# Casting a weight once into scratch inside an earlier phase, and emitting a conv and its transposes per channel chunk

## The reference

```python
xn = _layernorm(x)                       # x: (2, 4096, 2048)
q, k, v = xn@Wq.T+bq, xn@Wk.T+bk, xn@Wv.T+bv
q = dwconv3(q); k = dwconv3(k)           # depthwise, 3 taps along time
kv = k * v
y = irfft(rfft(kv) * rfft(ssm_kernel))   # long causal convolution
attn = ((y + kv*D_skip) * q) @ Wo.T + bo
h = xn @ W1.T                            # 2048 -> 8192
a = gelu(clip(round(h/0.1), -32768, 32767) * 0.1)
out = x + attn + a @ W2.T                # 8192 -> 2048
```

## Time and profile before

| | us |
|---|---|
| time, median of 2 runs | 5781.74 |
| the two runs | 5723.97 and 5839.51 |
| the profiled execution, its own time | 5727.18 |
| its span, slowest of 8 cores (core 4) | 5725.6 |
| spans of the other cores | 5682.0 to 5716.4 |

### The profile page before, as it was taken

How to read it: one execution, slowest core, us unless ns; L and a number is a source line. 1 busy time by engine, 2 the same in 40 slices (tenths; PEclk the granted TensorE clock), 3 DMA queues, 4 the chain that set the end, 5 groups by cost and what they waited for, 6 DMA issues and landing times. The chain is left out here.

```text
span 5725.6 us, 52508 instructions; the slowest of 8 cores (5682.0 to 5725.6 us)
## 1 busy us (share of the span) xinstructions
PE 3493.8 (61%) x18560; PEld 1797.6 (31%) x18560; DVE 1402.9 (25%) x2784; ACT 413.6 (7%) x791; POOL 652.0 (11%) x1212
## 2 busy tenths in 40 slices
PE   3777733999972602747747567514666666555644
PEld 1333312888861200323313223201222222221211
DVE  0111130445450210031031221310276673001011
ACT  0111100222220100000000000000111110000000
POOL 0000010111111000121121121200000001111111
PEclk9898966999986856979978889756899999988988
DMA  8777877122215014867857858341211112333333
GB/s 178 195 192 194 194 202 117 31 38 46 31 16 89 1 21 115 218 172 186 220 147 198 205 148 228 122 89 30 78 48 48 48 52 38 53 57 71 45 68 67
DMA packets 401726, 614.48 MB, mean 107 GB/s; under 512 B 228928, under 2 KB 283200, under 8 KB 371904
## 3 DMA queue, kind: packets, MB, share of 16 engines
q0 software_dynamic: 132320, 420.64, 35.1%
q1 hardware_dynamic: 269152, 190.48, 11.6%
HBM read 578.90 MB, written 138.94 MB: 125 GB/s over the span
## 5 line engine op out<-in xcount | busy, mean ns | idle before, releaser
L815 PE MATMUL ps<-p_kvg,p_tf 128*128 128x512 bf16 x3264 | 760.2, 393 | 523.9 <-DMA p_kvg<-kv_sp 294.7
L1103 PE MATMUL ps<-p_w,p_a 128*128 128x512 bf16 x2048 | 516.4, 400 | 390.5 <-DMA p_w<-w2T 274.0
L360 PE MATMUL ps<-p_ssm,p_tf 128*128 128x512 bf16 x2176 | 530.9, 409 | 241.6 <-ACT p_kb L377 152.6
L1047 PE MATMUL ps<-p_xn,p_w 128*128 128x512 bf16 x2048 | 476.0, 387 | 246.2 <-DVE p_u L1061 211.0
L815 PEld LDWEIGHTS ps<-p_kvg,p_tf 128*128 128x128 bf16 x3264 | 319.6, 100 | 964.1 <-issue 627.8
L533 PE MATMUL ps<-p_xq,p_wk 128*128 128x256 bf16 x3328 | 367.5, 273 | 183.0 <-DMA p_ckb<-ckb 183.0
L1103 PEld LDWEIGHTS ps<-p_w,p_a 128*128 128x128 bf16 x2048 | 192.0, 101 | 715.0 <-issue 549.4
L533 PEld LDWEIGHTS ps<-p_xq,p_wk 128*128 128x128 bf16 x3328 | 326.4, 98 | 222.4 <-issue 183.8
L360 PEld LDWEIGHTS ps<-p_ssm,p_tf 128*128 128x128 bf16 x2176 | 222.0, 104 | 550.0 <-issue 335.5
L533 PE MATMUL ps<-p_xq,p_wv 128*128 128x256 bf16 x3328 | 365.4, 273 | 0.0
L1047 PEld LDWEIGHTS ps<-p_xn,p_w 128*128 128x128 bf16 x2048 | 194.7, 99 | 527.6 <-issue 323.4
(11 more groups left out here) (80 smaller groups left out, 2272.6 us busy)
## 6 DMA issues: line engine op xcount, KB each, us to landing
p_tf<-tblf_sp POOLq DMA_DIRECT2D x136, 1024.0 KB, 7.5
tblf_sp<-p_tf SPq DMA_DIRECT2D x34, 1024.0 KB, 14.1
p_ti<-tbli_sp POOLq DMA_DIRECT2D x136, 256.0 KB, 2.9
p_wc<-w_lay POOLq DMA_DIRECT2D x128, 256.0 KB, 7.4
w_bf<-p_wc SPq DMA_DIRECT2D x128, 256.0 KB, 5.7
p_w<-w2T POOLq DMA_DIRECT2D x256, 128.0 KB, 3.2
p_x<-x_slab POOLq DMA_DIRECT2D x26, 1024.0 KB, 11.0
p_tf<-fwd_cos POOLq DMA_DIRECT2D x17, 1024.0 KB, 12.8
```

The costliest lines, as they stand in the source:

```text
L360: return E.matmul(bank(b)[:, :GSZ], tf[par][:, sc * 128:(sc + 1) * 128], ssm_sb[:, sc * D + gg * GSZ:sc * D + gg * GSZ + GSZ], start=(sc = ...
L815: return E.matmul(bank(b)[:, :GSZ], tf[par][:, pc * 128:(pc + 1) * 128], kvg[kp3][:, pc * GSZ:(pc + 1) * GSZ], start=(pc == g.PC0), stop=( ...
L1047: return E.matmul(bank(b)[:, :TJ], w1c[par][:, hc * 128:(hc + 1) * 128], xn[:, hc * NOWN + tj * TJ:hc * NOWN + (tj + 1) * TJ], start=(hc = ...
L1103: return E.matmul(bank(tc)[:, :EOSZ], a[:, fc * NOWN + tc * 128: fc * NOWN + tc * 128 + 128], w2c[par][:, :], start=(fc == 0), stop=(fc == ...
```

## The change

In phase 2b the convolution of chunk ec is recorded right after the matmuls of chunk ec, followed by the 8 transposes of that chunk and by two cast jobs (`emit_w2(2)`). After the loop the remaining cast jobs are emitted, then the drain. There are 64 x 2 = 128 jobs: each loads a 128x1024 piece of `w2T` with a cast on GpSimd's queue into one of two buffers and stores it to `w2_bf` on SyncE's queue. So 32 jobs stand in the loop and 96 behind it. In phase 5 the second product loads its 128x512 pieces from `w2_bf` instead of `w2T`, even chunks on GpSimd's queue and odd chunks on SyncE's. The rest of the diff binds a loop's function to its lambdas and moves a constant.

```diff
@@ _phase2b
+        CW2 = min(1024, D)
+        w2jobs = [(r, cc) for r in range(g.DFF // 128) for cc in range(D // CW2)]
+        w2state = {"n": 0, "val": {0: 0, 1: 0}}
+
+        def emit_w2(n):
+            for _ in range(n):
+                if not w2jobs:
+                    return
+                r, cc = w2jobs.pop(0)
+                wpar = len(w2jobs) % 2
+                if w2state["n"] >= 2:
+                    bld.wait(rec, "gpsimd", xWC[wpar], w2state["val"][wpar])
+                v = bld.dma(rec, "gpsimd", gWC[wpar], wcb[wpar][:, :CW2],
+                            env["w2T"][r * 128:(r + 1) * 128,
+                                       cc * CW2:(cc + 1) * CW2])
+                bld.wait(rec, "sync", gWC[wpar], v)
+                bld.dma(rec, "sync", xWC[wpar],
+                        env["w2_bf"][r * 128:(r + 1) * 128,
+                                     cc * CW2:(cc + 1) * CW2],
+                        wcb[wpar][:, :CW2])
+                w2state["val"][wpar] = bld.c[xWC[wpar]]
+                w2state["n"] += 1
...
-        bld.wait(rec, "vector", "A", ev_tok[job - 1])
-        CQ = min(512, NOWN)
-        qv = None
-        for ec in range(ECH):
+            bld.wait(rec, "vector", "A", ev_tok[job - 1])
             base = ec * QW
+            qv = None
             for jt in range(NOWN // CQ):
...
-        bld.wait(rec, "sync", "V", qv)
-        for tc in range(g.TCHO):
-            for ec in range(ECH):
+            bld.wait(rec, "sync", "V", qv)
+            for tc in range(g.TCHO):
                 bld.dma(rec, "sync", xQ,
                         env["qtm"][:, tc * D + ec * 128:tc * D + ec * 128 + 128],
                         qcv[:, ec * NOWN + tc * 128:ec * NOWN + tc * 128 + 128],
                         transpose=True)
+            emit_w2(2)
+        emit_w2(len(w2jobs))
         bld.drain(rec)
@@ _phase5
-    gW2 = [bld.dsem(f"p5gW2{i}", "gpsimd") for i in range(2)]
+    gW2 = [bld.dsem(f"p5gW2{i}", ("gpsimd", "sync")[i % 2]) for i in range(2)]
...
+                weng = ("gpsimd", "sync")[par % 2]
                 if fc >= 2:
-                    bld.wait(rec, "gpsimd", "T", w2_tok[(eo, fc - 2)])
+                    bld.wait(rec, weng, "T", w2_tok[(eo, fc - 2)])
...
-                v = bld.dma(rec, "gpsimd", gW2[par], w2c[par][:, :],
-                            env["w2T"][fc * 128:(fc + 1) * 128,
-                                       eo * EOSZ:(eo + 1) * EOSZ])
+                v = bld.dma(rec, weng, gW2[par], w2c[par][:, :],
+                            env["w2_bf"][fc * 128:(fc + 1) * 128,
+                                         eo * EOSZ:(eo + 1) * EOSZ])
                 bld.wait(rec, "tensor", gW2[par], v)
```

More of the change, by code:

```diff
@@ L610, in _phase2b @@
     xQ2 = bld.dsem("p2bxQ2", "sync")
+    gWC = [bld.dsem(f"p2bgWC{i}", "gpsimd") for i in range(2)]
+    xWC = [bld.dsem(f"p2bxWC{i}", "sync") for i in range(2)]
     with ExitStack() as P:
@@ L625, in _phase2b @@
         cqbs = sb("p2b_cqb", (128, ECH), F32)
+        wcb = [sb(f"p2b_wc{i}", (128, 1024)) for i in range(2)]
+        CW2 = min(1024, D)
[19 more added lines that the diff above has]
+                w2state["n"] += 1
         bld.dma(rec, "gpsimd", gB, wq.rearrange("p (hc e) -> p hc e", hc=ECH),
@@ L646, in _phase2b @@
         job = 0
+        CQ = min(512, NOWN)
+        QWT = ((QW + 15) // 16) * 16
         for ec in range(ECH):
@@ L652, in _phase2b @@
                     bld.wait(rec, "tensor", "A", ev_tok[job - 2])
-                QWT = ((QW + 15) // 16) * 16
                 def p2bmm(E, b, hc, ec, co, w):
@@ L663, in _phase2b @@
                     bld.run(rec, "tensor",
-                            lambda E, b=bnk, hc=hc, ec=ec, co=co, w=w:
-                            p2bmm(E, b, hc, ec, co, w))
+                            lambda E, b=bnk, hc=hc, ec=ec, co=co, w=w,
+                            f=p2bmm: f(E, b, hc, ec, co, w))
                 mt = bld.tok(rec, "tensor", "T",
-                             lambda E, b=bnk, ec=ec, co=co, w=w:
-                             p2bmm(E, b, ECH - 1, ec, co, w))
+                             lambda E, b=bnk, ec=ec, co=co, w=w, f=p2bmm:
+                             f(E, b, ECH - 1, ec, co, w))
                 bld.wait(rec, "scalar", "T", mt)
@@ L694, in _phase2b @@
                                                cvt[:, :CQ], OP.mult, OP.add))
[L696 to L705, removed]
-        bld.wait(rec, "sync", "V", qv)
-        for tc in range(g.TCHO):
-            for ec in range(ECH):
+                qv = bld.tok(rec, "vector", "V",
+                             lambda E, base=base, ec=ec, o=o:
+                             E.scalar_tensor_tensor(
+                                 qcv[:, ec * NOWN + o:ec * NOWN + o + CQ],
+                                 qpre[:, base + o + 2:base + o + 2 + CQ],
+                                 cqs[:, 2 * ECH + ec:2 * ECH + ec + 1],
+                                 cvt2[:, :CQ], OP.mult, OP.add))
+            bld.wait(rec, "sync", "V", qv)
+            for tc in range(g.TCHO):
                 bld.dma(rec, "sync", xQ,
@@ L1089, in _phase5 @@
                 par = fc % 2
+                weng = ("gpsimd", "sync")[par % 2]
                 if fc >= 2:
-                    bld.wait(rec, "gpsimd", "T", w2_tok[(eo, fc - 2)])
+                    bld.wait(rec, weng, "T", w2_tok[(eo, fc - 2)])
                 elif eo >= 1:
-                    bld.wait(rec, "gpsimd", "T", w2_tok[(eo - 1, FCH - 2 + fc)])
-                v = bld.dma(rec, "gpsimd", gW2[par], w2c[par][:, :],
-                            env["w2T"][fc * 128:(fc + 1) * 128,
-                                       eo * EOSZ:(eo + 1) * EOSZ])
+                    bld.wait(rec, weng, "T", w2_tok[(eo - 1, FCH - 2 + fc)])
+                v = bld.dma(rec, weng, gW2[par], w2c[par][:, :],
+                            env["w2_bf"][fc * 128:(fc + 1) * 128,
+                                         eo * EOSZ:(eo + 1) * EOSZ])
                 bld.wait(rec, "tensor", gW2[par], v)
```

## The result

The changed kernel is slower by 1.8%: the ratio of its time to that of the kernel before is 1.0178, with a 95% interval of 1.015 to 1.0207. The profiled execution took 5831.56 us against 5727.18 before, 104 us more; the forecast was 80 more, at 5807. In 14 of the 23 executions, 8 of 13 after and 6 of 10 before, one or both dies ran at a lower TensorE clock and took longer, among them the median of the 13, 5962.54 us, which lies above the forecast range of 5740 to 5895; the comparisons here use the others, or the other die. On those the sign was as forecast and the size near it, but the two large terms were both larger than forecast, and their misses partly cancel.

A forecast was written before the change was run, and what follows sets the result against it. The prediction took phase 2b's three barely overlapping jobs and the second product's waits for weight pieces as the limits. Phase 2b +182 (casts 377, interleaving 194) and the second product -102 turn 5727 into 5807 us, range 5740 to 5895.

The forecast's parts named there:

- a tail of over 370 us: Phase 2b: sign that the prediction is wrong, if the cast jobs after the loop take longer than this; 336 us was forecast.
- Interleaving, -194: Phase 2b: convolution and transposes overlap the matmuls, SyncE's queue sets the pace, transposes end at 2001 instead of 2195, saving 194 us.
- The 32 jobs in the loop, +41: Phase 2b loop: store issues on SyncE add 10 us and traffic slows the transposes by 31; the loop ends at 2042.
- Slowing by traffic: Phase 2b loop: cast loads and stores slow the transposes by 31 us (bounds 0 and 50), taken from phase 4.
- The 96 jobs behind the loop, +336: Phase 2b after the loop: nothing computes beside the casts, 3.5 us a job, 336 us (bounds 298 and 629).
- The 0.8 for sharing: Phase 2b tail: us added to a load-and-store cycle for the other buffer's use of the DMA engines, making 7.0.
- 0.2 for two wake-ups: Phase 2b tail: us a cycle added to a 4.0 us load and 2.0 us store, giving 6.2.
- The crowded tail: Rival, phase 2b: a job behind the loop takes 4.6 us instead of 3.5, another 106 us, total 5913; chance 0.22.
- The second product, -102: Phase 5: plain 128 KB loads land in 2.35 us instead of 3.2, a two-chunk cycle falls from 5.82 to 4.97; 102 us saved.
- The page's rule: Phase 5 loads: a DMA takes about 2.0 us plus bytes at 436 GB/s, so the saving would be about 36 us.
- Bytes only: Rival, phase 5: the load saves only its bytes, less 0.3 for a strided source; 38 us saved, total 5871; chance 0.11.
- Vanishing waits: Rival, phase 5: loads land in 1.9 us, the cycle is 4.5, 155 us saved, total 5754; chance 0.10.

## Why the prediction was right or wrong

**The sum was 80, and 104 was measured (on one core 130).** That it came so near is in part luck: the casts behind the loop cost 61 us more than forecast, the casts inside it 23 less, and the second product gave back 17 more. By its own sign, a tail of over 370 us, the prediction is wrong. The working had four terms.

**Interleaving, -194: right.** 188 were measured for it alone. The limit of the loop is SyncE's queue, as forecast: TensorE is done at 1973, the transposes at 2043.

**The 32 jobs in the loop, +41: they cost 18.** The loop was to take 204 us from its first transpose (1838 to 2042); it took 185.6 (1857.6 to 2043.2). That it ended within 2 us of the forecast is chance, since core 2 entered the stage 17 us later than core 4 in the earlier trace rows. Slowing by traffic was put at 31 us, and it was next to nothing: 167.4 us of transposes with the casts and without them. The stores with their gaps took 18 us instead of 10. The row from which the 31 came shows the difference. In phase 4 the casting load kept the engines of the core at 89.4%, and in those 54 us only 23 transposes started, where 44 did in the next 55; in the loop the DMA share was 0.49 to 0.58.

```profile
3757.48 54.49 SPq L196 DMA_TRANSPOSE p_y2fm<-y2tm  x23
...
q0 software_dynamic: 2057, 8.38, 89.4%
```

**The 96 jobs behind the loop, +336: the step that failed.** They took 397 on core 2 and 391 on core 4. The prices of a lone load and a lone store were right to the tenth (4.0 and 2.0, one buffer). What failed is what was laid on top. The 0.8 for sharing came from no row, and 0.2 for two wake-ups is little beside the 0.19 and 0.54 us that the prediction's own cycle of phase 5 has for two such steps. The prediction put 0.2 us for the wake-ups of a job and 0.8 a cycle for sharing, 7.0 in all. The runs show 0.6 to 0.7 for the wake-ups, and 1.3 us more for the load and 0.2 for the store when two chains run in step: 5.3 + 2.2 + 0.7 = 8.2. (The 5.3 is the median of all 128 loads; in the tail it is 5.2.) A row in hand gave a warning: 8192 KB of cast in 53.9 us is 1.7 us for 256 KB, near half of a load's 4.0, so the other buffer, the "only rival", was no small one. That the growth is this sharing and not HBM's is argued, as said above; that it comes from what runs beside the load is shown. The crowded tail was named as a rival from 3.86 us a job on; at 4.1 it came to pass in its mild form, though not for the reason it gave: there was no 1 MB table beside the jobs, and the landings stayed far from 7.4 and 5.7.

**The second product, -102: right in mechanism, short in size.** The median of eight cores is -119. The cycle fell by 0.73 to 0.77 us, less than the 0.85 forecast, as the load lands in 2.5 and not 2.35; by itself that is 93 to 99 us. The rest came from outside the sum: on core 4 the waits for the load fell by 84 us (274.0 to 190.1; 170 was forecast), and TensorE's busy time by another 40 (516.4 to 476.0), with the mean granted clock of the stage at 0.92 instead of 0.90. That part stood in no term, and why the clock was higher no run shows. The stage's clock before was 0.90 and not the 0.955 of the earlier trace rows, which leave out the stretches between the column blocks. And at 1.2 GHz the matmuls of a cycle, twice 3.78, are longer than the cycle of 5.82, so nothing would be saved there, not 0.3; that is worth 3 us. SyncE's loads were expected sooner than GpSimd's after a difference of 1.0 us at 512 KB; it is 0.2 to 0.3 at 128 KB (2.2 or 2.3 against 2.5). That they are nearly hidden was right: without the second queue the stage is 10 us longer.

**The page's rule.** By the Trainium skill, page "DMA: Bandwidth & Descriptors", section "Anatomy of one DMA — SWDGE (gpsimd) path", the saving would have been 0.3 us a cycle, as estimated from that page's formula; 0.73 to 0.77 was measured. The plain load's 2.5 us is near its 2.3, the casting load's 3.2 is not near its 2.6. A second rule of that page, section "Issuing engines are not separate DMA queues", says that issuing from several engines saves only the time it takes to initiate the DMAs; the run on one queue agrees, with about 10 us of 773.

**The rivals.** Bytes only: out, by 0.73 to 0.77 a cycle; its 0.3 for strided rows was read from no row, and the strided load landed 0.2 later than the contiguous one of the earlier trace rows. Vanishing waits: out for the change itself, 190 us of waits remain; four buffers brought them down to 9.4.

**What the change bought.** Of 307 us of gain (188 from interleaving, 119 in the second product) it paid back 397 in the tail and 18 in the loop, which leaves 108 lost where 104 was measured. All 128 casts cost 0 to 27 us in phase 2a, 17 on the slowest core, and 2 at most in the first product of phase 5. So the interleaving is good and the place of the casts is not. The stall that the casts are aimed at all but goes away with two more buffers of 1 KB a partition, and with these the casts bring nothing.

## What to carry to other kernels

Before a load is made shorter, ask whether it is waited for because of its length or because only two buffers stand against it: a cycle that reads "wait for the buffer, load, matmuls" is cured by more buffers, and then the length no longer matters as long as it fits: here 3.7 us against the 5.2 us of the three chunks in the other buffers. Work that is cheap beside other work costs its full length behind a drain; look for the stretch where the limiting engine is busy and the DMA share low, and record the queue's urgent transfers ahead of it. When a ping-pong of loads and stores is priced, take each transfer's share of the DMA engines too: two chains did not halve the time here (4.1 us a job against 6.67), where a load needs the engines for near half of its own 4.0 us.

## What the runs showed that was not expected

- A casting load of 256 KB takes as much as 1.85 us of all 16 DMA engines alone and 2.05 beside another, a plain store of 256 KB 0.67 to 0.68 (shares of the queues times the time of a job). With four buffers the engines are 89% busy at 3.0 us a job.
- From the landing of one transfer to the issue of the one that waits for it, load to store to load, a chain loses 0.6 to 0.7 us a job.
- Transposes of 128x128 keep a pace of 1.31 us beside matmuls and VectorE, and no slower one beside two casting loads and two stores for each 8, at a DMA share of 0.49 to 0.58; beside a single load that kept the engines at 89% they ran at half the pace.
- Moved beside matmuls that keep TensorE busy, 96 MB of HBM traffic (64 read, 32 written) cost 0 to 27 us in 679, by the core.
